# Waits for a first part, the credits moved from SyncE to TensorE, and new tables of places in a four-layer block kernel

## The reference

```python
x = x + _L0_attn_ref(_layernorm(x), ...)   # attention in windows of 128, 16 heads, then a GELU MLP of width 1024
x = x + _L0_ffn_ref(_layernorm(x), ...)    # RWKV channel mix: r * (relu(k)**2 @ W_v)
x = x + _L1_attn_ref(_layernorm(x), ...)   # Mamba: in_proj, convolution of 4 taps, scan with 512 x 16 states, out_proj
x = x + _L1_ffn_ref(_layernorm(x), ...)    # one of 8 experts for each sequence, picked by the mean of its rows
```

## Time and profile before

| | us |
|---|---|
| median of three runs | 3150.91 |
| the profiled execution | 3158.34 |
| its span, first to last instruction | 3156.5 |
| PE busy | 2776.2 |
| POOL busy | 2640.5 |
| DVE busy | 2502.5 |
| ACT busy | 2397.7 |

### The profile page before, as it was taken

The page is one execution under the profiler, slowest core; times in us unless marked ns, Lnnn a source line. Parts: engine busy times, 40 slices in busy tenths (PEclk is TensorE's granted clock), DMA queues, the critical chain, the costliest instruction groups (busy, mean ns, idle before and its releaser), DMA issues.

```text
span 3156.5 us, 54604 instructions
## 1 busy us (share of the span) xinstructions
PE 2776.2 (88%) x17328; PEld 1765.1 (56%) x17328; DVE 2502.5 (79%) x5644; ACT 2397.7 (76%) x5299; POOL 2640.5 (84%) x1590
## 2 busy tenths in 40 slices
PE   4788788899999999999899899999999899978657
PEld 3555445465565656566565656656565655654326
DVE  3256988889797978889797988979788897989970
ACT  4677878888796978878797888879798787965432
POOL 1116999999998999999999999999899989988870
PEclk9899999999999999999999999999999999999778
DMA  3005353545445454644545464544646454465541
GB/s 84 14 11 168 124 170 98 194 146 186 146 147 195 142 195 144 220 136 138 179 155 192 129 228 144 158 160 145 209 126 214 142 180 152 147 195 189 175 125 42
DMA packets 285967, 477.31 MB, mean 151 GB/s; under 512 B 38451, under 2 KB 93363, under 8 KB 285683
## 3 DMA queue, kind: packets, MB, share of 16 engines
q1 hardware_dynamic: 285682, 473.83, 46.0%
HBM read 388.79 MB, written 84.93 MB: 150 GB/s over the span
## 4 chain that ended last, share of the span: by engine, by line
PE 59%; POOL 17%; DVE 9%; issue 8%; ACT 5%; DMA 1%; SPq 1%; DVEq 0%; POOLq 0%; ACTq 0%
PE bank L765 19%; PE bank L773 8%; POOL h_rows L1786 8%; POOL h_rows L1796 7%; PE bank L1024 6%; PE bank L1010 6%; PE bank L963 5%; PE bank L810 4%; PE bank L888 3%; PE bank L798 3%; PE bank L826 3%; DVE h_rows L1562 2%; PE bank L759 2%; DVE prob L1345 2%; ACT prob L1079 1%
## 5 line engine op out<-in xcount | busy, mean ns | idle before, releaser
L1786 POOL TENSOR_TENSOR h_rows<-u_rows,b_rows 128x1024 f32<-128x1024 f32 x512 | 1203.4, 2370 | 23.2 <-DMA b_rows<-bc_dram 19.4
L1796 POOL TENSOR_TENSOR h_rows<-h_rows,c_rows 128x1024 f32<-128x1024 f32 x480 | 1128.5, 2366 | 76.3 <-DVE state L1569 47.0
L1250 ACT ACTIVATE bank<-d_rows,a_rep 128x512 f32<-128x512 f32 x1024 | 682.2, 689 | 222.6 <-DVE v_pad L1372 82.7
L1562 DVE TENSOR_TENSOR_SCAN h_rows<-bank,state,h_rows 128x512 f32<-128x512 f32 x480 | 593.7, 1269 | 47.6 <-ACT bank L1250 42.5
L1562 DVE TENSOR_TENSOR_SCAN h_rows<-bank,h_rows 128x512 f32<-128x512 f32 x480 | 573.0, 1212 | 63.2 <-ACT bank L1250 46.5
L1079 ACT ACTIVATE prob<-prob,neg_max 128x256 f32<-128x256 f32 x1024 | 510.2, 505 | 36.0 <-DVE neg_max L1345 35.9
L1345 DVE CUSTOM_DVE_ANT_0 prob<-bank,bands 128x256 f32<-128x256 f32 x896 | 336.6, 419 | 122.0 <-PE bank L798 75.4
L810 PE MATMUL bank<-ident,prob 128*128 128x128 f32 x2048 | 330.8, 287 | 87.7 <-ACT prob L1079 55.0
L810 PEld LDWEIGHTS bank<-ident,prob 128*128 128x128 f32 x2048 | 237.5, 144 | 273.4 <-issue 140.3
L963 PE MATMUL bank<-h_rows,sum_n 128*32 128x512 f32 x2048 | 298.0, 662 | 74.3 <-POOL h_rows L1796 55.9
L1010 PE MATMUL bank<-y4T,w 128*128 128x256 f32 x1024 | 250.9, 392 | 12.7 <-DMA e_b<-in_b 10.8
(11 more groups left out here) (164 smaller groups left out, 4852.9 us busy)
## 6 DMA issues: line engine op xcount, KB each, us to landing
u_rows<-u_dram SPq DMA_DIRECT2D x256, 256.0 KB, 3.9
d_rows<-delta_dram SPq DMA_DIRECT2D x256, 256.0 KB, 4.1
b_rows<-bc_dram SPq DMA_DIRECT2D x256, 256.0 KB, 3.1
c_rows<-bc_dram SPq DMA_DIRECT2D x256, 256.0 KB, 3.2
w<-in_W SPq DMA_DIRECT2D x28, 1024.0 KB, 6.8
zs_dram<-region_b SPq DMA_DIRECT2D x64, 256.0 KB, 3.7
xc_dram<-region_b SPq DMA_DIRECT2D x64, 256.0 KB, 2.7
u_dram<-region_b SPq DMA_DIRECT2D x64, 256.0 KB, 5.0
```

The costliest lines, as they stand in the source:

```text
L1250: e.activation(banks[at.bank][:, :], d_rows[:, c, :], ACT.Exp, scale=a_rep[:, k:k + 1]).then_inc(filled[at.bank], 1)
L1562: e.tensor_tensor_scan(rows, banks[at.bank][:, :], rows, start, ALU.mult, ALU.add).then_inc(drained[at.bank], 1)
L1786: e.tensor_tensor(half_of(i, b, half), u_rows[:, 2 * half:2 * half + 2, :], twice(b_rows[:, b % 2, :]), ALU.mult).then_inc(bx_ready.sem, 1)
L1796: e.tensor_tensor(rows, rows, twice(c_rows[:, b % 2, :]), ALU.mult).then_inc(hc_ready.sem, 1)
```

## The change

It does five things. First, products wait for their parts one by one. Second, SP's 102 increments go to PE, and SP no longer passes through `constants`. Third, `constants` no longer waits for the first weights and `s_diag`; the few steps that need them wait there themselves, at i = 0 alone, and DVE's L2112 moves behind the first two norms. Fourth, `VECTOR_QUADS` replaces `LAST_QUADS`: scan 15 keeps its eight quads on DVE, scan 14 has five (1, 4, 7, 10, 13) where it had eight. Fifth, nearly all numbers of `PLACES`, `THREADS` and `LEADS` are new; a line of them:

```diff
 PLACES = {
     "head": (
-        -1295, -228, -174, 428, 922, 922,
+        -1622, -446, -340, 345, 925, 1156,
     ),
...
-MIDDLE_QUADS, LAST_QUADS = (), tuple(range(1, QUADS, 2))
-
-
-def vector_quads(i, batches):
-
-    return LAST_QUADS if i >= 2 * batches - 2 else MIDDLE_QUADS
+VECTOR_QUADS = 14 * ((),) + ((1, 4, 7, 10, 13), tuple(range(1, QUADS, 2)))
...
-        def pe_product_T(e, use, lhsT, rhs, parts, rows=P):
+        def pe_product_T(e, use, lhsT, rhs, parts, rows=P, ready=()):
             e.wait_ge(*free(use))
             for n in range(parts):
+                if ready:
+                    e.wait_ge(*ready[n])
                 ins = e.matmul(banks[use.bank][0:rows, :], lhsT(n), rhs(n), start=(n == 0), stop=(n == parts - 1))
...
-            e.wait_ge(*gone(use("t1.0")))
-            e.wait_ge(*gone(use("t1.1")))
+            if i == 0:
+                e.wait_ge(s_w, 16 * len(WEIGHTS))
             for m, name in enumerate(("q0", "q1", "k0", "k1")):
-                pe_product_T(e, use(name), lambda n: w_qkv[:, n, m * P:(m + 1) * P], lambda n: nT[:, n, :], KD)
+                pe_product_T(e, use(name), lambda n: w_qkv[:, n, m * P:(m + 1) * P], lambda n: nT[:, n, :], KD,
+                             ready=() if m else (gone(use("t1.0")), gone(use("t1.1"))))
...
-            e.wait_ge(*hidden.at(i, 2))
             for t in range(GT):
                 at = use(f"m{t}")
                 e.wait_ge(*free(at))
                 for k in range(KF):
+                    if t == 0 and k % 4 == 0:
+                        e.wait_ge(*hidden.at(i, k // 4 + 1))
...
-                for j in range(KM // 2):
-                    e.wait_ge(*gone(uses["expert", i, f"e{half}.{j}"]))
...
                     for k in range(KM):
+                        if j == 0 and k % 2 == 0:
+                            e.wait_ge(*gone(uses["expert", i, f"e{half}.{k // 2}"]))
...
+            if i == 0:
+                e.wait_ge(s_w, 16 * len(WEIGHTS))
+                for mu in ("mu_r", "mu_k"):
+                    ins = e.tensor_scalar(col["not_" + mu], col[mu], -1.0, 1.0, ALU.mult, ALU.add)
+                ins.then_inc(s_diag, 1)
             yield from range(7)
             e.wait_ge(*carry_in.at(i))
...
         def constants(e):
-            e.wait_ge(s_w, 16 * len(WEIGHTS))
             e.wait_ge(s_pool, 1)
             e.wait_ge(s_dve, 3)
-            e.wait_ge(s_diag, 1)
...
         @block.sync
         def _(e):
-            for s in sems:
-                e.sem_inc(s.sem, CREDIT * s.step)
-            for n in range(8):
-                e.sem_inc(filled[n], CREDIT)
-                e.sem_inc(drained[n], CREDIT)
             e.dma_start(x_in[:, :, :], x_view[0]).then_inc(x_landed.sem, 16)
...
-            constants(e)
             run(e, "sync", head=sp_head, attention=sp_attention, mlp=sp_mlp, rwkv=sp_rwkv, middle=sp_middle,
...
-            e.wait_ge(s_w, 16 * len(WEIGHTS))
             e.wait_ge(s_pool, 1)
-            for mu in ("mu_r", "mu_k"):
-                e.tensor_scalar(col["not_" + mu], col[mu], -1.0, 1.0, ALU.mult, ALU.add)
...
         @block.tensor
         def _(e):
+            for s in sems:
+                e.sem_inc(s.sem, CREDIT * s.step)
+            for n in range(8):
+                e.sem_inc(filled[n], CREDIT)
+                e.sem_inc(drained[n], CREDIT)
             constants(e)
```

More of the change, by code:

```diff
@@ L103 @@
 THREADS = (
[L104 to L110, removed]
+    (("head", "attention",), (-3974, -1637, -1878, -1870, -1843, -1868, -1867, -1885, -1885, -1885, -1880, -1894, -1879, -1910, -1895, -1945)),
+    (("mlp", "rwkv", "middle",), (-1651, -1880, -1865, -1845, -1870, -1870, -1894, -1887, -1887, -1881, -1881, -1896, -1894, -1889, -1938, -2018)),
+    (("scan",), (-1895, -1834, -1840, -1862, -1868, -1872, -1863, -1885, -1885, -1873, -1870, -1900, -1887, -1923, -1988, -1472)),
+    (("back",), (-1837, -2394, -2397, -1869, -1867, -1832, -1866, -2324, -1884, -1879, -1813, -1858, -2062, -2104, -1875, 313)),
+    (("route",), (1155, -1746, -4346, -1889, -3024, -1590, -1913, -2076, -1979, -1976, -2720, -1774, -1790, -1961, 1979, -289)),
+    (("fetch",), (-2607, -2351, -2014, -2042, -1482, -1852, -2404, -1657, -929, -1904, -1933, -1440, -2236, 713, 997, 5025)),
+    (("expert",), (-1821, -1853, -1867, -1875, -1873, -1873, -1941, -1876, -1884, -1885, -1889, -1952, -2008, -3026, 6197, 8482)),
 )
@@ L117 @@
         "head": (
[L118 removed]
+            72, 476, 86, 107, -128, -292,
         ),
         "attention": (
[4 rows of a table removed]
[4 rows of a table added]
         ),
         "mlp": (
[L127 to L128 removed]
+            -191, -32, -273, -380, -495, -51, -25, 61, -220, -8, 252, -212, 165, -147, 202, -87, -25, 148, 144, -677,
+            -1170, -59, -251, -136, -184, -125, 174, 522, 538, -59,
         ),
         "rwkv": (
[L131 removed]
+            -1, 42, -59, 40, -83, -89, 7, 74, -93, 0, 0, -38, -38, -38, 0, -80, -88, -49, -2, 0,
         ),
         "middle": (
[L134 to L135 removed]
+            8, -259, -95, 122, -77, -515, 27, -304, -191, -252, -61, -268, 0, -399, -157, 48, -79, -224, -391, -360,
+            -678, -714, 11, -259, -29, -253, 97, -167, -301,
         ),
         "scan": (
[7 rows of a table removed]
[7 rows of a table added]
         ),
         "back": (
[L147 removed]
+            -550, 86, 76, -13, 253, -244, -64, -251, 99, 437,
         ),
         "route": (
[L150 removed]
+            -28, 5, 27,
         ),
         "fetch": (
[L153 removed]
+            -255,
         ),
         "expert": (
[L156 removed]
+            0, 158, 0, -233, 21, -625, -4, 403, -152, 58, 54, 0, 0, 0, 0, 0, 0, -317, -460, 125, 41, 457, 211, 226,
+            0,
         ),
@@ L160 @@
         "head": (
-            20, 74, 215, 285, 51, 51,
+            217, 430, 576, 0, 0, 0,
         ),
         "attention": (
[5 rows of a table removed]
[5 rows of a table added]
         ),
         "mlp": (
-            621, 381, -184, 187, -467, -365, -890, -900, -688, -592, -451, -129, -156, 0, -68, 0, 228, 248, 248, 248,
-            0, 0, 0, 0, -7, 0, 16, 0, 0, 543,
+            234, 232, -263, 0, -285, -169, -9, 188, -77, -526, 0, 0, 0, 0, 0, 210, 0, 0, 0, 0, 0, 0, 0, 0, 0, 0, 0,
+            0, -327, 493,
         ),
         "rwkv": (
-            -101, -155, -26, -176, 18, -235, -42, -42, 0, 379, 571, 314, 14, -74, 6, -44, -1, -19, -207, 0,
+            151, -63, 14, -169, 0, -279, -167, -331, 44, 266, 15, 192, 66, 15, -41, 0, 80, -356, -220, 38,
         ),
         "middle": (
-            0, 279, 0, 0, 84, 172, 0, -41, -133, -599, 14, 80, 0, 0, -125, -177, 82, -48, 75, -121, 180, -17, 352, 0,
-            -346, -808, 260, -445, 0,
+            167, 412, -27, 116, 84, 172, 70, 0, -133, 0, 14, 57, -22, -149, -22, -280, 4, -51, 67, -66, -8, 0, 183,
+            42, -955, -901, 258, 0, 0,
         ),
         "scan": (
[7 rows of a table removed]
[7 rows of a table added]
         ),
         "back": (
-            -76, 232, -106, 30, 18, -1020, 139, 170, 170, 68,
+            -295, 166, -133, -210, 11, -1368, -11, 624, 800, -590,
         ),
         "route": (
-            0, -187, 0,
+            178, 136, -448,
         ),
         "fetch": (
-            174,
+            834,
         ),
         "expert": (
-            -199, -276, 0, 0, 0, -44, -283, 91, 104, 91, -307, -27, -160, 11, 41, -47, -695, -18, -210, -210, 110,
-            67, 93, 299, 909,
+            577, 141, -2, -332, -659, 322, 717, 341, -9, 23, 1, 24, 0, -61, 696, 595, 335, 0, 611, -167, 94, 212, 96,
+            300, -438,
         ),
@@ L295 @@
         "head": (
-            60, 423, 729, 823, -158, 1734,
+            146, 370, 864, 942, -28, -257,
         ),
         "attention": (
[5 rows of a table removed]
[5 rows of a table added]
         ),
         "mlp": (
-            0, 0, -599, -331, -95, 147, -56, -78, -507, -726, -767, -767, -804, -1348, -2000, -2000, -1941, -653,
-            -904, 351, -1134, -927, -755, -918, -799, -951, -2000, -789, -1185, -1505,
+            0, 0, 0, 0, 0, 0, 0, 0, 0, 0, 0, 0, 0, 0, 0, 155, 155, 155, 155, 155, 155, 155, 155, 155, 0, 0, 0, 0, 0,
+            0,
         ),
         "rwkv": (
-            -1842, -538, -538, -1547, -392, 161, 259, 237, 237, 257, 257, -196, 655, 294, 279, 692, 841, 729, 544,
-            279,
+            0, 0, 0, 0, 0, 0, 0, 0, 0, 0, 0, 0, -83, -83, -83, 0, -13, 0, 0, 0,
         ),
         "middle": (
-            582, -91, -304, 52, -63, 183, -460, 0, 0, 0, 214, 214, -87, 37, 209, 203, 354, 451, 451, 199, -44, -4,
-            -4, 24, 156, 156, -334, -108, -377,
+            544, 544, 544, 0, 0, 46, -3, -3, -3, -3, -3, -3, -3, 0, 0, 0, 0, 0, 0, 0, 150, 150, 150, 0, 0, 0, 0, 78,
+            0,
         ),
         "scan": (
[8 rows of a table removed]
[7 rows of a table added]
         ),
         "back": (
-            273, 683, 683, -338, -338, -219, -177, 4, -177, -177,
+            212, 0, 0, -11, -239, -102, 347, 304, 0, 708,
         ),
```

(30 more changed lines are left out.)

69 lines of the change are left out of this document (34 added, 35 removed), and 152 rows, old and new, of tables (LEADS, PLACES).

## The result

The changed kernel takes 3196.97 us, median of four runs (3191.13 to 3199.55), beside 3152.18 for the kernel before on the same chip (four runs): a ratio of 1.0135, 95% interval 1.0117 to 1.0152. It is 45 us slower; 3132 was forecast, with a range up to 3156. The profiled execution took 3191.13 us, the shortest of the four, that of before 3158.34, so that the two traces differ by 33 of the 45.

What follows compares the result with a forecast made beforehand. PE and POOL, busy 170.06 and 169.28 of 181.00 us, bound the steady period; DVE decides scan 14. −11.0 − 5.6 − 6 + 4 = −18.6 takes the median 3150.91 to 3132 us, range 3114 to 3156.

Steps and rivals of the forecast that it cites:

- the steady state: Middle periods: most table swaps cost nothing; three exceptions, reload +5, norm +5, attention −6, together +4 us.
- The sign that the prediction gave for this: Steady period, 181 us: the prediction is wrong if it changes by more than 1 us.
- the one on the slower side: Rival: POOL's 4.3 us stalls ahead of `rstd_c` count in full, 39 instead of 5, giving 3166 us; chance 0.12.
- The start, −11.0: Kernel start: first DMA at about 0.75 us without increments, first norm at about 5.9 instead of 16.91, 11.0 us gained.
- the lower bound: Start: loads go out no sooner, rows land at 11.56, the norm starts at 11.8 us, a gain of 5.1.
- The first parts, −5.6: Expert products at the end: gaps of 4.7 us go, plus 0.92 once in the fill.
- Scan 14, −6: Scan 14: five quads on DVE instead of eight shift work to POOL; stretch of 152.0 becomes about 145, 6 us taken.
- The lower bound, 0: Scan 14: no gain if the chain into scan 15 does not move with DVE's work.
- The reload, +5: MLP weights' reload on SP comes later; PE waits 1.0 us in ten groups, 10 in all, 5 taken.
- The norm, +5: Behind the scan: POOL waits 4.3 us for `shift_c`, 3.24 swallowed, 1.1 left in nine groups, 9.9; 5 taken.
- Attention, −6: Every second group: PE's 1.97 us wait for ACT is covered by `rwkv` transposes, six times, 11.8 us; half taken.

Runs made afterwards that it cites:

- e7: e3 with the 102 increments put back from PE to SP, ahead of its first DMA; 3136.67 us, ratio 0.9945.
- e4: e1 with eight quads on DVE in scan 14 instead of five; 3128.19 us, ratio 0.9916.
- e6: e4 with the output's store and the reload of the MLP's weights put back on SP where the kernel before had them; 3128.07 us, ratio 0.9915.
- e5: e4 with the norm behind the scan put back behind POOL's two products with B, groups 0 to 12; 3129.45 us, ratio 0.9926.
- e1: Changed kernel with ACT's wait for the expert's first weights put directly ahead of the first instruction needing them; 3133.28 us, ratio 0.9937.
- e3: Changed code with the kernel before's PLACES, THREADS and LEADS, and eight quads in both last scans; 3133.11 us, ratio 0.9938.

## Why the prediction was wrong

The step that failed is the sentence on the steady state: "Most swaps of the tables are of neighbours that wait for nothing. Three are not". There was a fourth. I had compared lists of instructions; the expert's step 0 on ACT is a wait without an instruction, so it moved in none of those lists, and its +62 stands nowhere in the sum. The sign that the prediction gave for this came: the steady period, 181 us, was to change by no more than 1, and two of the three shown grew by 9 and 6. Among the rivals, the one on the slower side gave 39 us to POOL's wait ahead of `rstd_c`, the wrong wait on the wrong engine. Put right by that single wait, the kernel takes 3133.28, and 3132 was forecast; but that is partly luck, as the terms show:

- **The start, −11.0:** right, 11.4 at the first norm. With the increments on SP the norm stands at 11.50 (e7), where the lower bound had 11.8. In e7 102 increments on SP hold the first DMA by 6.5 us, 64 ns each; on PE they hide, as said. The Trainium skill's page "Advanced Engine Details and Errata" (section "DMA Bandwidth Details") gives an increment of a semaphore about one cycle, in a list on DMA transfers; for increments that are instructions of SP, e7 does not agree. That the start counts whole is not shown: of the 5.95 us that e7's norm is later, 4 are left after scan 1.
- **The first parts, −5.6:** right, 5.9 at the end. The four gaps of the earlier trace rows, 4.7 together, are gone, and a pair of products takes 13.8 us from start to start instead of 15.2. The first product behind a transpose waits 0.17 us instead of 0.92.
- **Scan 14, −6:** wrong, 0. The step was "With the idle time that DVE has today, 152.0 − 141.0 = 11": the idle time of one engine was added to the busy time of another. POOL's own is 18.0, and DVE's grew too (e4 above). The lower bound, 0, held.
- **The reload, +5:** 2.4 us of waiting at PE's products in four groups, where waits in ten groups were forecast; putting it back changes nothing (e6).
- **The norm, +5:** POOL does wait, 36 to 39 us in nine or ten groups, and putting the norm back gains nothing (e5). I had let 3.24 of 4.3 us be swallowed; as far as the times tell, it was everything.
- **Attention, −6:** the six waits of 1.97 us are gone, and PE waits two steps earlier instead, at L793 for ACT's `z`, six times, 2.0 at most, 11.4 in all (e1). No gain shows: e1 with the new tables and e3 with the old ones take the same.

Together these give −11.4 − 5.9 with 0 for the rest, −17.3 instead of −18.6. e1 and e3 lie 21 us below the kernel before; of the remaining 4 us, 3 would lie in the fill by e3's trace, and where the rest belongs is not shown.

Why could ACT's 11 us not be absorbed, when POOL's 4 could? The prediction had put the price on new waits of PE and POOL alone, since ACT is idle for some 30 us of a period. The waits suggest the answer, which no run tests by itself. POOL's wait for `shift_c` held only POOL, shortly before it would have waited for DVE anyway. ACT stands between all the others: its `prob` ends DVE's wait for `rden`, DVE's `rden` ends POOL's, and PE's next bank is drained by ACT. Of two engines that are each busy for 170 of 181 us, both stood still, 7.5 and 6.7 us in the case shown.

## What to carry to other kernels

In a kernel whose order is written out, compare the lists of waits, not only of instructions: a step that only waits moves without a trace in the instruction list and holds everything behind it, here 6 to 11 us in ten groups, for weights that nothing needed yet. Put a wait directly ahead of its first user, so that no table can move the two apart. And when idle time before an instruction is released by something that the instruction doesn't read, look in the code for a wait that stands between two stages.

## What I had not expected of the hardware

The same instructions take different times from run to run, and the granted clock goes with it over whole runs: of the five runs of e4 the shortest took 3122.7 us at a mean granted clock of 0.955, the longest 3133.8 at 0.950. The 23.7 us by which the changed kernel was ahead after scan 1 are partly this spread: e1 has the same instructions in the same order up to there and was 17.1 ahead. Between 60 and 150 us its granted clock was 0.87, with some 24 us at 1.2 GHz and the rest at 2.4, where the changed kernel's profile had 0.92 and some 14 us; that this accounts for all of the 6.6 us is not shown. So a difference of 5 us between two of these versions, as between e1 and e4, is no more than one version shows between its own runs.
